# One explicit drain on GpSimd between its last load and the experts' part

## The chip, the cores and the metric

One NeuronCore of a Trainium2 chip runs the whole kernel in one launch. The metric is the device time of one execution in microseconds (us). The engines are named as the profile names them: PE (TensorE), DVE (VectorE), ACT (ScalarE), POOL (GpSimd) and SP (SyncE, which here only issues DMAs). Each engine has its own stream of instructions, and a letter q behind a name (POOLq, SPq) means the engine's sequencer: the part that reads the stream, waits on semaphores and issues DMAs.

## The reference

Eight sequences of 128 tokens with 512 features pass through one decoder layer with three parts, each followed by a layer norm without weights:

```python
x = layernorm(x + self_attention(x, Wq, Wk, Wv, Wo))      # 32 heads of 16, 8 groups, RoPE, causal
x = layernorm(x + cross_attention(x, ctx, mask, bias, ln_weight, w_q, w_k, w_v, w_out))
                                                          # 32 heads of 128; it adds x once more itself
x = layernorm(x + ffn(x))
# ffn: y = x @ W_base.T + b_base
#      + sum over 4 active experts e of alpha_e * 2 * (x @ A_e.T) @ B_e.T      (rank 8)
#      alpha = softmax(log(prior) + x @ router_W.T + router_b) over the active ones
```

## The kernel before, in words

Self-attention comes first (`self_attention`, up to L753), one sequence after the other. Cross-attention follows in 16 groups of two heads (`NG = 16`): groups 0 and 1 are written out, groups 2 to 14 (`SEVEN = 2`) are a hardware loop on each engine, and group 15 is written out again as the last one. Then comes the third part, called the experts here: the final norm of cross-attention, the base product and the low-rank experts, the last layer norm, and one store of 256 KB for each of the eight sequences.

There is no scheduler. Each engine's stream stands in the order of the Python code of its own function (`sync`, `gpsimd`, `scalar`, `vector`, `tensor` of each part), and the streams meet only in semaphores: `wait_ge(sem, n)` holds a stream until the count is reached. `nc.Block()` (opened in L909, recorded under L771) ends all five streams with the same closing sequence: each engine runs a DRAIN, tells a common semaphore, and waits until all five have arrived. An opening sequence of the same form stands before the first instruction (recorded under L2411).

What POOL does, in its order:

- In self-attention: fills, subtractions, small norm arithmetic, and two DMAs, L363 (x into `acc`) and L364 (half of the context into `stage`).
- In each group of cross-attention: four additions of bias and mask (`bias_mask`, L1048, into `bm`), four subtractions on weights (`three_turns`, `last_turn`), and seven loads of 1 MB from a scratch tensor in HBM into one of two ring buffers (`load_sums`). A load waits until PE has used what lies in the ring buffer, runs a tiny addition on the tile `pool_gate` (L1077), and issues the DMA (L1078). The loops over groups 2 to 15 issue 96 such DMAs in all.
- In the last group only `first_half(NG - 1)` is left (L1283, defined in L1263): three loads (S4k, S3q, S3k) and the additions of bias and mask for the tiles 2 and 3. The last of these, the second L1048, is POOL's last instruction in cross-attention. POOL issues no DMA after that.
- In the experts (L1284 to L1300): `rstd_x` (L1170, L1173), `add_bias` (L1178) and `rstd_y` (L1182, L1184, L1187), all of them short. The last store (L1037, issued by SP) waits for DVE's L1890, which waits for the last L1184.

SP issues all other DMAs: the weights, the bias, the experts' inputs and the eight stores. Behind them it waits until all stores have landed (L1038), and then enters the closing sequence.

Of the kernel before, what the change touches and what calls it, by code (L numbers as in the profile page):

```python
# [763 lines left out]
def layer(nc, a, sem, banks, mem, prev_a, out_d):  # L764
# [6 lines left out]
    with ExitStack() as ctx:  # L771
# [75 lines left out]
        def wait_kept(eng, name):  # L847
            i = BLOCKS.index(name)
            eng.wait_ge(s_kept[i % 2], 32 * (i // 2 + 1))
# [191 lines left out]
        def _(pool):  # L1041
            def bias_mask(g, s, first):
                n, i = TILES * g + s, heads_of(first)[s]
                if s == 0:
                    pool.wait_ge(s_bias_in, 16 * g + 16)
                if not first or s >= 2:
                    pool.wait_ge(s_nm, n - 1)
                nc.gpsimd.tensor_tensor(bm[:, s % 2], mask[:, HALF * (s // HG):HALF * (s // HG + 1), :],  # L1048
                                        bias[:, i:i + 1, :].broadcast_to([P, HALF, T]), ALU.add)\
                    .then_inc(s_bm, 1)  # L1050
# [22 lines left out]
            def load_sums(g, name, w=None, after=None):  # L1073
                k = SLOT_OF[name]
                if after is not None:
                    pool.wait_ge(s_unit[w], done(UNITS, g, after))
                    nc.gpsimd.tensor_tensor(pool_gate[:, BLOCKS.index(name):BLOCKS.index(name) + 1], eps[:, 0:1], eps[:, 0:1], ALU.add)  # L1077
                nc.gpsimd.dma_start(mem.ring[k][:].rearrange("p q c n -> p (q c n)"), sums_d[BLOCKS.index(name)])\  # L1078
                    .then_inc(s_ring[k], 16)
# [88 lines left out]
            def rstd_x(p):  # L1168
                pool.wait_ge(e_mvx, 2 * p + 2)
                nc.gpsimd.tensor_tensor(rstx[:, 2 * p:2 * p + 2], mvx[:, 2 * p:2 * p + 2, 1], eps[:], ALU.add)\  # L1170
                    .then_inc(e_vex, 1)
                pool.wait_ge(e_vex, p + 1)
                nc.gpsimd.tensor_tensor(rstx[:, 2 * p:2 * p + 2], rstx[:, 2 * p:2 * p + 2], minus_half[:], ALU.pow)\  # L1173
                    .then_inc(e_rx, 1)
# [81 lines left out]
            def second_half(g):  # L1256
                bias_mask(g, 0, False)
                last_turn(g)
                bias_mask(g, 1, False)
                load_sums(g, "S1k", 0, "p6")  # L1260
                load_sums(g, "S4q", 1, "p6")

            def first_half(g):  # L1263
                load_sums(g, "S4k", 1, "p5")
                bias_mask(g, 2, False)
                wait_kept(pool, "S4q")
                load_sums(g, "S3q", 0, "p3")
                load_sums(g, "S3k", 1, "p3")
                bias_mask(g, 3, False)
# [7 lines left out]
            with pool.Fori(SEVEN, NG - 1) as g:  # L1277
# [3 lines left out]
                load_sums(g, "S2q", 1, "p7")  # L1281
                second_half(g + 1)
            first_half(NG - 1)  # L1283
            pool.wait_ge(s_experts_in, 16 * len(EXPERT_INPUTS))  # L1284
            rstd_x(0)
            add_bias(0)
# [1134 lines left out]
```

## Time and profile before

| | |
|---|---|
| median of 3 runs | 1077.29 us (1076.80 to 1078.42) |
| the profiled execution, its own time | 1079.05 us |
| span of that execution in the trace | 1076.8 us |
| granted TensorE clock over the span, mean | 0.992 of full speed |
| PE / PEld / DVE / ACT / POOL busy | 96% / 83% / 71% / 46% / 44% |
| DMAs issued by POOL (queue q0) | 103.82 MB in 14240 packets |
| DMAs issued by SP (queue q1) | 54.37 MB in 30560 packets |

The span is what lies between the first and the last recorded instruction. The profiled execution's own time is 2.25 us longer than its span. The busy times on the page leave out register, branch, semaphore and drain instructions. Those are found by asking for the source line under which they were recorded. The answers give their times from the start of the span.

### The profile page before, as it was taken

How to read it: one execution, taken by the hardware profiler on the slowest of the kernel's cores; microseconds unless marked ns; L12 is line 12 of the kernel's file. 1: busy time of each engine (PE TensorE's matmuls, PEld its weight loads, DVE VectorE, ACT ScalarE, POOL GpSimd, SP SyncE). 2: the span in 40 equal slices, each digit the busy share in tenths (PEclk: the TensorE clock that was granted, in tenths of full speed). 3: DMA queues.
4: the chain of work that ended last, by engine and by line, in shares of the span. 5: the costliest groups of instructions: out<-in, count | busy, mean ns of one | idle time of the engine just before them, and what ended most of it. 6: DMA issues, size and time to landing. Idle time of an engine off the chain costs nothing.

```text
span 1076.8 us, 20565 instructions
## 1 busy us (share of the span) xinstructions
PE 1030.2 (96%) x6354; PEld 894.6 (83%) x6354; DVE 761.8 (71%) x2269; ACT 500.6 (46%) x1377; POOL 472.6 (44%) x567
## 2 busy tenths in 40 slices
PE   7899988999989999999999999999999999999995
PEld 6678767888778888888888888988888888988884
DVE  5799989664747676757677676767676767577883
ACT  4888886453424343534443434444343434343421
POOL 7676676599934232423324242424242424232242
PEclk9999999999999999999999999999999999999998
DMA  4302001235265556473737464646465564736001
GB/s 153 128 12 60 2 1 66 80 126 195 69 227 185 177 180 215 140 238 125 253 135 238 148 222 159 223 170 213 147 217 180 176 221 135 239 110 248 5 20 59
DMA packets 44845, 158.72 MB, mean 147 GB/s; under 512 B 4737, under 2 KB 21505, under 8 KB 32129
## 3 DMA queue, kind: packets, MB, share of 16 engines
q0 software_dynamic: 14240, 103.82, 28.0%
q1 hardware_dynamic: 30560, 54.37, 15.0%
q8 instruction: 22, 0.36, 0.1%
q14 instruction: 23, 0.18, 0.1%
HBM read 148.73 MB, written 9.44 MB: 147 GB/s over the span
## 4 chain that ended last, share of the span: by engine, by line
PE 79%; DVE 10%; issue 4%; POOL 3%; ACT 2%; DMA 2%; POOLq 0%; SPq 0%; DVEq 0%; ACTq 0%
PE bank L1946 25%; PE bank L760 20%; PE bank L2108 16%; PE bank L2095 5%; PE bank L2078 5%; PE bank L2126 3%; PE bank L2085 2%; DVE sm L481 2%; DMA ring<-block_sums 1%; POOL sm L322 1%; DVE alpha L557 1%; DMA stage<-in_wq 1%; ACT pr L1339 1%; PE bank L2164 1%; PE bank L686 1%
## 5 line engine op out<-in xcount | busy, mean ns | idle before, releaser
L1339 ACT ACTIVATE pr<-sm,nmx 128x128 f32<-128x128 f32 x256 | 99.8, 391 | 176.2 <-DVE nmx L1594 172.7
L1048 POOL TENSOR_TENSOR bm<-mask,bias 128x512 f32<-128x512 f32 x64 | 84.5, 1321 | 162.3 <-DVE nmx L1594 159.7
L1644 DVE TENSOR_TENSOR acc<-acc,bank 128x512 f32<-128x512 f32 x128 | 86.2, 684 | 80.1 <-PE bank L2108 80.1
L1077 POOL TENSOR_TENSOR pool_gate<-eps 128x1 f32<-128x1 f32 x95 | 37.6, 396 | 239.5 <-PE bank L1946 239.5
L1946 PE MATMUL bank<-ring,wqk_hi 128*128 128x512 f32 x392 | 111.0, 405 | 7.1 <-DVE wqk_lo L1612 4.1
L1612 DVE TENSOR_TENSOR wqk_lo<-qk_raw,wqk_hi 128x512 fp32r<-128x512 f32 x98 | 106.2, 1085 | 8.5 <-ACT wqk_hi L1369 8.5
L1332 ACT COPY v<-bank 128x256 f32<-128x256 f32 x124 | 45.9, 370 | 128.6 <-PE bank L760 81.8
L2108 PE MATMUL bank<-wo_hi,at_hi 128*128 128x512 f32 x256 | 101.2, 395 | 0.3 <-DVE acc L1644 0.3
L2108 PE MATMUL bank<-wo_hi,at_lo 128*128 128x512 f32 x256 | 100.5, 392 | 0.5 <-DVE at_lo L1606 0.5
L2108 PE MATMUL bank<-wo_lo,at_hi 128*128 128x512 f32 x256 | 100.6, 393 | 0.0
L1606 DVE TENSOR_TENSOR at_lo<-bank,at_hi 128x512 fp32r<-128x512 f32 x64 | 44.0, 688 | 64.5 <-ACT at_hi L1353 64.5
L760 PE MATMUL bank<-wv_hi,cT_hi 128*128 128x256 f32 x512 | 88.8, 296 | 0.2 <-DVE wv_lo L1901 0.2
L760 PE MATMUL bank<-wv_lo,cT_hi 128*128 128x256 f32 x512 | 82.3, 283 | 0.0
L760 PE MATMUL bank<-wv_hi,cT_lo 128*128 128x256 f32 x512 | 82.2, 283 | 0.0
L1946 PEld LDWEIGHTS bank<-ring,wqk_hi 128*128 128x128 f32 x392 | 67.1, 190 | 16.6 <-issue 5.1
L760 PEld LDWEIGHTS bank<-wv_hi,cT_hi 128*128 128x128 f32 x512 | 72.7, 190 | 4.6 <-issue 0.4
L1347 ACT COPY prT<-bank 128x512 f32<-128x512 f32 x64 | 37.2, 582 | 81.4 <-PE bank L2085 81.4
L2078 PEld LDWEIGHTS bank<-kT,qT 128*128 128x128 f32 x512 | 66.7, 191 | 4.8
L760 PEld LDWEIGHTS bank<-wv_hi,cT_lo 128*128 128x128 f32 x512 | 70.5, 191 | 0.0
L760 PEld LDWEIGHTS bank<-wv_lo,cT_hi 128*128 128x128 f32 x512 | 70.4, 191 | 0.0
L2095 PE MATMUL bank<-prT,v 128*128 128x128 f32 x512 | 67.8, 275 | 1.6 <-ACT prT L1347 1.6
L2078 PE MATMUL bank<-kT,qT 128*128 128x128 f32 x512 | 67.3, 274 | 0.0
(296 smaller groups left out, 2611.1 us busy)
## 6 DMA issues: line engine op xcount, KB each, us to landing
ring<-block_sums POOLq DMA_DIRECT2D x96, 1024.0 KB, 5.2
qk_raw<-in_wqk SPq DMA_DIRECT2D x56, 256.0 KB, 5.3
o_raw<-in_wo SPq DMA_DIRECT2D x16, 512.0 KB, 3.3
v_raw<-in_wv SPq DMA_DIRECT2D x15, 512.0 KB, 4.5
block_sums<-stage SPq DMA_DIRECT2D x6, 512.0 KB, 4.1
acc<-in_x POOLq DMA_DIRECT2D x1, 2048.0 KB, 8.1
qk_raw<-in_wqk SPq DMA_DIRECT2D x4, 512.0 KB, 6.3
bias<-in_bias SPq DMA_DIRECT2D x16, 128.0 KB, 2.1
```

The source lines that it names most:

```text
L760: ins = nc.tensor.matmul(out, lhs, rhs, start=start and i == 0, stop=i == len(pairs) - 1)
L1048: nc.gpsimd.tensor_tensor(bm[:, s % 2], mask[:, HALF * (s // HG):HALF * (s // HG + 1), :], bias[:, i:i + 1, :].broadcast_to([P, HALF, T]), ...
L1077: nc.gpsimd.tensor_tensor(pool_gate[:, BLOCKS.index(name):BLOCKS.index(name) + 1], eps[:, 0:1], eps[:, 0:1], ALU.add)
L1332: nc.scalar.copy(v[:, b, :], PX[b % 2][:, 0:HG * DH2]).then_inc(s_vc, 1)
L1339: e = nc.scalar.activation(pr[:, s % 2, k], sm[:, s % 2, k], ACT.Exp, bias=nmx[:, s % 2, k:k + 1], accum_out=sums[:, s % 2, k:k + 1])
L1606: nc.vector.tensor_tensor(at[1][:, s // HG, i], PO[:], f32(at[0][:, s // HG, i]), ALU.subtract).then_inc(s_al, 1)
L1612: nc.vector.tensor_tensor(part_of(slot, 1), block_of(qk_raw, raw), f32(part_of(slot, 0)), ALU.subtract).then_inc(s_op, 1)
L1644: nc.vector.tensor_tensor(acc[:, b], acc[:, b], PX[b % 2][:], ALU.add).then_inc(s_acc, 1)
L1946: ins = nc.tensor.matmul((PQ, PK)[w][:], lhs, rhs, start=i == 0, stop=i == len(pairs) - 1)
L2078: ins = nc.tensor.matmul(S[s % 2][:, tok], qT[:, s % 2, tok], kT[:, s % 2, tok], start=True, stop=True)
L2095: ins = nc.tensor.matmul(PO[:, k * T:(k + 1) * T], v[:, half * HALF + k, i * DH2:(i + 1) * DH2], prT[:, k], start=True, stop=True)
L2108: ins = nc.tensor.matmul(PX[b % 2][:], at[p][:, half, i, tok], wo[q][:, i, :], start=k == 0 and (p, q) == PARTS[0], stop=k == HG - 1 and ( ...
```

## The change

One instruction is added to POOL's stream: a DRAIN with no semaphore of its own. It stands behind the last addition of bias and mask of the last group, and ahead of the first wait of the experts.

```diff
@@ -1281,6 +1281,7 @@
                 load_sums(g, "S2q", 1, "p7")
                 second_half(g + 1)
             first_half(NG - 1)
+            pool.drain()
             pool.wait_ge(s_experts_in, 16 * len(EXPERT_INPUTS))
             rstd_x(0)
             add_bias(0)
```

All other instructions of all five streams, with their waits, stay as they are and in their order. The lines behind L1283 move down by one number.

## Rows read from the trace of the kernel before

**Rows 1.** The page: busy us, share and count of each engine; then the chain's shares.

```profile
PE 1030.2 (96%) x6354; PEld 894.6 (83%) x6354; DVE 761.8 (71%) x2269; ACT 500.6 (46%) x1377; POOL 472.6 (44%) x567
...
PE 79%; DVE 10%; issue 4%; POOL 3%; ACT 2%; DMA 2%; POOLq 0%; SPq 0%; DVEq 0%; ACTq 0%
```

**Rows 2.** The chain of waits, its last pieces: start us, us, what.

```profile
1065.37 0.45 PE bank L2176 x2
...
1067.06 0.20 POOL rstd_y L1182
...
1067.33 0.55 POOL rstd_y L1184
...
1067.92 0.59 POOLq L771
```

**Rows 3.** Line 771, the closing sequence: duration ns min/median/max, first and last start.

```profile
L771 POOLq EVENT_SEMAPHORE  x2: 17/17/17, 1076.6 to 1076.7; - x2
L771 PEldq DRAIN  x1: 2720/2720/2720, 1063.1 to 1063.1; - x1
L771 ACTq DRAIN  x1: 844/844/844, 1065.1 to 1065.1; - x1
L771 POOLq DRAIN  x1: 8684/8684/8684, 1067.9 to 1067.9; - x1
L771 DVEq DRAIN  x1: 589/589/589, 1067.9 to 1067.9; - x1
L771 SPq COMPARE_BRANCH  x1: 38/38/38, 1070.5 to 1070.5; - x1
L771 SPq DRAIN  x1: 13/13/13, 1070.7 to 1070.7; - x1
L771 SPq EVENT_SEMAPHORE  x1: 17/17/17, 1076.8 to 1076.8; - x1
...
L771 PEldq EVENT_SEMAPHORE  x1: 51/51/51, 1076.8 to 1076.8; - x1
```

**Rows 4.** Timeline of all engines from 1067 us: start us, us, engine, instruction.

```profile
1067.91 0.55 DVE L1890 TENSOR_SCALAR acc<-v_raw,mv_y,rstd_y 128x512 f32<-128x512 f32 x1 [0.94 <-POOL rstd_y L1184]
1067.97 0.53 POOL L1187 TENSOR_SCALAR minus_mean_rstd<-mv_y,rstd_y 128x1 f32<-128x1 f32 x1
1068.48 0.33 SPq L1037 DMA_DIRECT2D out<-acc  x1
```

**Rows 5.** Busy time of each engine by window, with clock, DMA share, GB/s.

```profile
1068.50:1070.70 2.20, 0.00 (x0) 0.00 (x0) 0.00 (x0) 0.00 (x0) 0.00 (x1) 0.85 0.32 119
1070.70:1076.60 5.90, 0.00 (x0) 0.00 (x0) 0.00 (x0) 0.00 (x0) 0.00 (x0) 0.50 0.00 0
```

**Rows 6.** Line 2411, the opening sequence, as in rows 3.

```profile
L2411 POOLq DRAIN  x1: 168/168/168, 0.3 to 0.3; - x1
...
L2411 POOL MEMSET const-uint8-127<- x1: 101/101/101, 0.3 to 0.3; 128x1 uint8 x1
```

**Rows 7.** Lines that issue DMAs, one by one: the form of rows 3.

```profile
L1078 POOL DMA_DIRECT2D ring<-block_sums x96: 577/577/613, 294.2 to 985.0; - x96
...
DMA to landing us min/median/max: 5.0/5.2/9.3
...
L363 POOL DMA_DIRECT2D acc<-in_x x1: 758/758/758, 43.7 to 43.7; - x1
...
L364 POOL DMA_DIRECT2D stage<-in_cT x1: 789/789/789, 44.5 to 44.5; - x1
...
L1037 SPq DMA_DIRECT2D out<-acc x8: 332/333/1570, 1044.9 to 1068.5; - x8
...
DMA to landing us min/median/max: 2.0/2.0/3.4
```

**Rows 8.** POOL's timeline around the place of the change; idle before it in brackets.

```profile
990.37 1.29 POOL L1048 TENSOR_TENSOR bm<-mask,bias 128x512 f32<-128x512 f32 x1 [4.81 <-DVE nmx L1594]
1014.71 0.19 POOL L1170 TENSOR_TENSOR rstd_x<-mv_x,eps 128x2 f32<-128x2 f32 x1 [23.05 <-DVE mv_x L1651]
```

**Rows 9.** The windows behind that place: columns as in rows 5.

```profile
991.70:999.80 8.10, 8.10 (x49) 7.00 (x48) 6.67 (x20) 4.10 (x13) 0.00 (x0) 1.00 0.57 209
999.80:1014.70 14.90, 13.37 (x91) 11.78 (x89) 11.22 (x34) 7.91 (x21) 0.00 (x0) 1.00 0.00 0
```

**Rows 10.** Line 1187, POOL's change of configuration in the experts: as rows 3.

```profile
L1187 POOLq MODIFY_POOL_CONFIG  x2: 11/11/11, 1040.1 to 1040.1; - x2
```

## The prediction

> **What bounds the kernel now.** I read the page's busy table and its chain first [rows 1]. PE is busy for 96% of the span and carries 79% of the chain, so for most of the kernel POOL's time is worth nothing: POOL is busy 44% and carries 3%. The reader should then follow the chain to its end and notice that it ends too early [rows 2]. Its last piece is POOLq at L771, from 1067.92 for 0.59 us, that is to 1068.51. The span ends at 1076.8. So 8.3 us at the end are explained by no compute row.
>
> That stretch belongs to the closing sequence, and the view of line 771 opens it [rows 3]. Five engines run a DRAIN and then meet. I add start and duration. PE is through at 1063.1 + 2.72 = 1065.8, ACT at 1065.1 + 0.84 = 1065.9, DVE at 1067.9 + 0.59 = 1068.5, and SP at 1070.7 + 0.01 = 1070.7. POOL starts at 1067.92 (the start of the last chain piece) and takes 8.684 us, to 1076.60. The meeting's semaphore instructions follow at 1076.6 to 1076.8, and that is the end. All engines are idle from 1068.5 on, and from 1070.7 to 1076.6 no byte moves [rows 5]. POOL's closing DRAIN alone holds the end for those 5.9 us.
>
> What is POOL doing in it? Its last instruction, L1187, runs from 1067.97 for 0.53 us, to 1068.50 [rows 4]. The other 8.10 us of the DRAIN (1076.60 minus 1068.50) pass with nothing of POOL's in progress. The opening DRAIN on the same engine took 168 ns, and it began beside a fill of 101 ns, both at 0.3 us [rows 6]; between 0.07 and 0.17 us of it was its own. Between the two, POOL issued 96 + 1 + 1 = 98 DMAs [rows 7]. SP issued many DMAs too, and its closing DRAIN took 13 ns, so it is POOL's kind of DMA that would count. So the trace offers one difference between the long DRAIN and the short ones: DMAs issued by POOL since the previous DRAIN. An estimate from it is 8.10 / 98 = 0.083 us for each. All of them had landed long before: the last was issued at 985.0 and the slowest of L1078 took 9.3 us [rows 7], so by 994.3. The 8.10 us would then be bookkeeping for DMAs, not waiting for data.
>
> **The change part by part.** It removes nothing, moves nothing, and adds one DRAIN on POOL.
>
> Its place: the addition ahead of it ends at 990.37 + 1.29 = 991.66, and POOL's next instruction starts at 1014.71, after 23.05 us of waiting for DVE's mv_x [rows 8]. Queued behind the DRAIN on POOL is that `rstd_x(0)` and with it everything in the experts. DVE waits for its result, and PE for DVE's. So the new DRAIN costs nothing as long as it is shorter than 23.05 us, and each us above that goes to the end one for one. Bounds of its length: below, 0.17 us (the opening one); above, by the nearest rows, 2.7 us until the slowest DMA has landed (994.3 minus 991.66) and 8.10 us of its own, 10.8 us in all. I take 8.1 us, since the same 98 DMAs stand before it. It then ends at about 999.8, with 14.9 us to spare, and the cover is the last group's work on PE and DVE [rows 9]. If that cover shrank by more than 14.9 us, the cost would begin to show.
>
> What it gives: the closing DRAIN has no POOL DMA since the previous DRAIN. Bounds of what is left of it after L1187: 0.07 us at the least (the opening DRAIN's 0.17 us less the fill beside it), 8.10 us at the most (nothing changes). I take under 0.17 us, nearest to the opening DRAIN, which had the same state: POOL arrives at about 1068.50 + 0.17 = 1068.7. Late next is SP. Its last store is issued at 1068.48 [rows 4] and takes 2.0 us to land [rows 7], so SP goes on at 1070.5 and finishes its DRAIN at 1070.7 [rows 3]. The end is then SP's, and POOL may keep up to 2.2 us of DRAIN (1070.7 minus 1068.5) without cost. Behind the last arrival come the meeting's own steps: 1076.8 minus 1076.6, 0.2 us [rows 3]. SP has to signal POOL first, where now POOL is the last itself, so I allow 0.1 us more.
>
> The sum against the profiled execution: new end 1070.7 + 0.3 = 1071.0 in place of 1076.8, a change of -5.8 us; the time goes from 1079.05 to 1073.25. The median of the runs is 1.76 us below the profiled execution, and the DRAIN is no work that depends on data, so I take the same difference there: 1077.29 - 5.8 = 1071.5 us.
>
> Could the 5.9 us be an effect of the profiler, absent in timed runs? The timed runs are only 1.76 us shorter than the profiled one. So at most that much of it could be missing from them if the rest is equal, and the gain would still be over 4.0 us.
>
> Two rules of the Trainium skill speak against a gain. The page "VectorE: DVE Perf Modes", section "The DRAIN you can't avoid", describes the drains at the two ends of a kernel as a constant of about 12 ns on all five engines. SP's 13 ns agrees; POOL's 8684 ns does not [rows 3], and the measurement decides. By that rule there would be nothing to take from the end, and the time would stay at 1077.3 us.
>
> The page "PSUM — Partial Sum Buffer", section "Engine vs sequencer instructions", says that a drain waits until its engine is fully idle. By that alone POOL would be through at 1068.5 [rows 4], 8.1 us before it is. So the trace does not agree here either, unless POOL is at work on something that has no row.
>
> **The rivals.**
>
> *No change: the 8.1 us are paid at the close in any case.* The long DRAIN differs from the opening one in more than its DMAs. It comes after 567 POOL instructions, and after a change of POOL's configuration at 1040.1 [rows 10], behind the place of the new DRAIN. If the price is one for the first DRAIN after such a change, or a fixed price once POOL has issued any DMA, the closing DRAIN stays at 8.7 us. The new one is hidden in 23.05 us either way, and the time is 1077.3 us. Against it: the compute instructions after that change ran at once, the first within 0.2 us (L1187 is 0.26 to 0.53 us in all its rows), and an engine with nothing to account for has no reason to be busy for 8 us. A rule behind this rival stands in the Trainium skill's page "GPSIMD Engine Reference", section "Instruction dispatch": the first call to freshly loaded code pays about 6 us that no row shows. No row here shows such a gap behind 1040.1.
>
> *A part only.* Some of the 8.1 us stays with the close. Up to 2.2 us of rest changes nothing; a rest of 4 us would end at 1072.5 + 0.2, and the time would be about 1073.2 us. Nothing in the trace points to a split.
>
> *Slower: the new DRAIN does its work beside DVE and holds DVE up.* At the close all other engines are idle, so rows 5 cannot show whether it disturbs them. At its new place DVE is busy for 6.67 of 8.10 us and PE for all 8.10 [rows 9]. If DVE could not run for the whole DRAIN, PE would wait for up to 8.1 us, and the sum is 8.1 - 5.8 = +2.3, 1079.6 us. The point from which it decides is 5.8 us of added time on that chain. Against it: the DRAIN has no tile to read or write, and additions of 1.3 us on POOL with two inputs each run beside DVE throughout the kernel.
>
> **How the numbers follow.** A measurement of this kernel tells 0.2% (2.15 us) from no change. The forecast, 1071.5 us, has 0.80. It is the only reading in which the sole difference in the rows matters, and it needs only that three quarters of the 8.1 us move. A part only has 0.04. No change has 0.12, because the trace holds only one long DRAIN and I can't separate its causes. Slower has 0.04. Faster by over 0.2%: 0.80 + 0.04 = 0.84; within 0.2%: 0.12; slower: 0.04. The low end takes the end at SP's arrival with the 0.2% by which two series of runs can differ: 1071.2 - 2.1 = 1069.1. The high end takes the gain of 4.0 us if the profiler has lengthened the DRAIN, 1073.3, and the partial case with some of the same spread: 1074.4. That leaves out no change and slower, 0.16.
>
> **What would show it.** Right: line 771 shows a POOLq DRAIN of about 0.6 to 0.8 us instead of 8.684, with POOL's semaphore instructions at about 1070.8; the new drain's line shows a POOLq DRAIN of about 8 us from about 990.4 or 991.7; `rstd_x` at L1170 (now one line further down) still starts at about 1014.7, released by DVE; PE's last product ends where it did, at 1065.8. Wrong: two long DRAINs (the price is fixed); a short new one and a long closing one (the cause lies behind 990); wider gaps on PE between 992 and 1015 (contention).

## The result, and the profile after

The changed kernel takes 1072.1 us in the median of 5 runs (1071.17 to 1072.34), against 1077.29 us for the kernel before (5 runs as well, with the same median as the 3 above). The ratio is 0.995, with a 95% interval from 0.9935 to 0.9964, so it is clear of 1. A second series on one chip gave 0.9944 [0.9931, 0.9957]. The profiled execution took 1072.06 us with a span of 1069.9 us.

The closing sequence, line 771, in the changed kernel answers to [rows 3]. Columns: duration in ns min/median/max, first and last start.

```profile
L771 POOLq EVENT_SEMAPHORE  x2: 17/17/17, 1069.7 to 1069.8; - x2
L771 PEldq DRAIN  x1: 2718/2718/2718, 1062.1 to 1062.1; - x1
L771 ACTq DRAIN  x1: 844/844/844, 1064.0 to 1064.0; - x1
L771 POOLq DRAIN  x1: 664/664/664, 1066.9 to 1066.9; - x1
L771 DVEq DRAIN  x1: 586/586/586, 1066.9 to 1066.9; - x1
...
L771 SPq DRAIN  x1: 13/13/13, 1069.6 to 1069.6; - x1
L771 SPq EVENT_SEMAPHORE  x1: 17/17/17, 1069.8 to 1069.8; - x1
```

POOL's closing DRAIN is down from 8684 to 664 ns. SP is now the last to arrive, and 0.2 us later all is over. From the start of PE's closing DRAIN to the end it took 1076.8 - 1063.1 = 13.7 us before and takes 1069.9 - 1062.1 = 7.8 us now: 5.9 us less.

The new DRAIN in the same trace (line 1284), then POOL's timeline around it, which answers to [rows 8]. The code behind the change stands one line further down.

```profile
L1284 POOLq DRAIN  x1: 9432/9432/9432, 989.1 to 989.1; - x1
```

```profile
989.13 1.29 POOL L1048 TENSOR_TENSOR bm<-mask,bias 128x512 f32<-128x512 f32 x1 [4.80 <-DVE nmx L1595]
1013.63 0.19 POOL L1170 TENSOR_TENSOR rstd_x<-mv_x,eps 128x2 f32<-128x2 f32 x1 [23.21 <-DVE mv_x L1652]
```

The DRAIN begins beside the addition, which ends at 990.42, and is through at 989.1 + 9.43 = 998.6. Its own part is 8.1 us, as long as what the closing DRAIN had paid. `rstd_x` is still released by DVE.

The span fell by 6.9 us, 1.0 us more than the end explains. At the addition L1048, ahead of the new DRAIN, the changed kernel is already 990.37 - 989.13 = 1.2 us early. The five runs of the same kernel have spans from 1069.0 to 1070.2 us, so this is within their scatter. The traces show where the scatter sits. These are the sixteenth of the 64 additions of bias and mask, in the kernel before and then in the changed one:

```profile
379.97 1.28 POOL L1048 TENSOR_TENSOR bm<-mask,bias 128x512 f32<-128x512 f32 x1 [4.08 <-DVE nmx L1594]
...
378.74 1.28 POOL L1048 TENSOR_TENSOR bm<-mask,bias 128x512 f32<-128x512 f32 x1 [4.09 <-DVE nmx L1595]
```

The 1.2 us are there already. From this addition to the last one it is 990.37 - 379.97 = 610.40 us before and 989.13 - 378.74 = 610.39 us now. In all other traces below whose loads are as they were, and that have no DRAIN between these two additions, it is 610.38 to 610.40 us too, while the sixteenth starts anywhere from 377.5 to 380.0 us. So a cost or a gain late in the kernel can be read from such stretches to a few hundredths of a microsecond, and better than from the whole time.

Did the DRAIN disturb its neighbours? This is the window of its 8.1 us in the changed kernel, against the first of [rows 9]. Columns: busy us of PE, PEld, DVE, ACT, POOL, then clock, DMA share, GB/s.

```profile
990.42:998.56 8.14, 8.14 (x48) 6.95 (x47) 6.52 (x20) 3.99 (x12) 0.00 (x1) 1.00 0.57 207
```

PE is busy throughout in both and DVE does 20 instructions in both, in 6.52 us now and 6.67 us before. DMAs moved 207 GB/s and 209 GB/s. From the start of the addition to `rstd_x` it takes 1014.71 - 990.37 = 24.34 us before and 1013.63 - 989.13 = 24.50 us now. Two of the kernels below have no DRAIN in this stretch either, and it takes 24.37 and 24.58 us in them. So no delay by the DRAIN shows.

### The profile page after: what moved, and what is told of

Same layout as the page of the kernel before. It is cut to its first block, busy times and chain, and to the rows that moved or that the text cites. A ratio compares the mean times of both kernels' runs of the same rounds, so it can differ in the third digit from the quotient of the medians.

```text
span 1069.9 us, 20566 instructions
## 1 busy us (share of the span) xinstructions
PE 1028.4 (96%) x6354; PEld 893.1 (83%) x6354; DVE 760.8 (71%) x2269; ACT 501.1 (47%) x1377; POOL 473.0 (44%) x567
## 4 chain that ended last, share of the span: by engine, by line
PE 78%; DVE 10%; issue 5%; POOL 3%; ACT 2%; DMA 1%; POOLq 0%; DVEq 0%; ACTq 0%
PE bank L1947 25%; PE bank L760 20%; PE bank L2109 16%; PE bank L2096 5%; PE bank L2079 5%; PE bank L2127 3%; PE bank L2086 2%; DVE sm L481 2%; DMA ring<-block_sums 1%; POOL sm L322 1%; DVE alpha L557 1%; ACT pr L1340 1%; PE bank L2165 1%; PE bank L686 1%; DVE mn L481 1%
## 5 line engine op out<-in xcount | busy, mean ns | idle before, releaser
L1048 POOL TENSOR_TENSOR bm<-mask,bias 128x512 f32<-128x512 f32 x64 | 85.0, 1329 | 162.1 <-DVE nmx L1595 159.5
```

## The experiments

All of them start from the kernel before, unless the edit says otherwise. Where a DRAIN's own part is given, it is its duration less what still ran of the instruction ahead of it. For the closing one that is L1187 or its like, which ends 0.59 us after the DRAIN begins. The diffs are cuts, and some of the code in them is shortened.

### One DRAIN pays, the next does not

```diff
+            pool.drain()
             pool.drain()          # the changed kernel, with a second one
```

> Two DRAINs in a row at the place of the change. Theory (a DRAIN pays about 0.083 us for each POOL DMA issued since the previous one): the first takes 8.1 us of its own (about 9.4 with the addition of 1.29 us ahead of it), the second under 0.2 us, the closing one 0.66 us as after the change, and the time is that of the changed kernel, 1072 us. Rival (a fixed price of each DRAIN once POOL has issued DMAs, which the closing one escapes for another reason): the second takes 8 us too, still within the 23 us of waiting.

Its single run took 1070.8 us. The two DRAINs, lines 1284 and 1285:

```profile
L1284 POOLq DRAIN  x1: 9432/9432/9432, 987.9 to 987.9; - x1
...
L1285 POOLq DRAIN  x1: 47/47/47, 997.4 to 997.4; - x1
```

The second costs 47 ns. There is no fixed price of each DRAIN; there is a debt, and the first one clears it.

### The same DRAIN at the end saves nothing

```diff
             for b in range(2, B):
                 rstd_y(b)
+            pool.drain()
```

> The same DRAIN, but as POOL's last instruction, behind the last rstd_y. Theory (the work is moved, not saved): the explicit DRAIN takes 8.1 us of its own behind POOL's last instruction, the closing one under 0.2 us, and the end is where it was before the change: 1077.3 us, ratio 1.000. Rival (any additional DRAIN makes the closing one short and costs little itself): 1072 us, ratio 0.995.

1077.32 us, ratio 1.000 [0.9988, 1.0013]. Lines of the closing sequence, and the explicit DRAIN (line 1301):

```profile
L771 SPq DRAIN  x1: 13/13/13, 1068.7 to 1068.7; - x1
L771 POOLq DRAIN  x1: 47/47/47, 1074.7 to 1074.7; - x1
...
L1301 POOLq DRAIN  x1: 8682/8682/8682, 1066.0 to 1066.0; - x1
```

The explicit one takes what the closing one took before, 8682 against 8684 ns, and SP waits for it as before. What gains is the place, not the instruction.

### 95 DMAs ahead of the DRAIN, 3 behind it

```diff
+            pool.drain()
             first_half(NG - 1)
```

> The DRAIN stands ahead of the three loads of the last group, with 95 DMAs issued before it and 3 behind it. Theory per DMA: the explicit one takes 95 x 0.083 = 7.9 us of its own; POOL has about 4.4 us of waiting there (the gap ahead of S4k), so that load and what uses it come 3 to 4 us late, and the closing DRAIN pays for 3 DMAs, 0.25 us behind L1187, still ahead of SP. Time: between 1072 us (PE does not need the load at once) and 1076 us. Rival (a fixed price whenever any POOL DMA is outstanding): the closing DRAIN is 8.7 us again and the time 1077 to 1081 us.

1074.82 us, ratio 0.9982 [0.9969, 0.9995]. The two DRAINs, then where PE waits, then the windows around it:

```profile
L771 POOLq DRAIN  x1: 908/908/908, 1069.3 to 1069.3; - x1
...
L1283 POOLq DRAIN  x1: 9061/9061/9061, 968.7 to 968.7; - x1
```

```profile
PE bank L1947 <- DMA ring<-block_sums: 2.9, 1, 2.9
```

```profile
980.50:983.45 2.95, 0.03 (x1) 0.00 (x1) 0.00 (x0) 0.37 (x1) 0.32 (x1) 1.00 1.05 397
983.45:987.40 3.95, 3.95 (x10) 3.13 (x11) 1.31 (x5) 0.00 (x0) 0.71 (x2) 0.57 0.51 193
```

The closing DRAIN is 908 ns here and 664 ns in the changed kernel. The difference, 0.24 us, is the price of the 3 DMAs behind the explicit DRAIN: 0.081 us each. The explicit one ends at 968.7 + 9.06 = 977.7, and the issue ahead of it at 969.3. So its own part for 95 DMAs is 8.4 us, where 7.9 us were expected: half a microsecond more, directly behind a load just issued. It delays the load S4k, PE waits 2.9 us for it, and in the next 4 us its granted clock is 0.57, near the lower of its two levels, after a stretch with hardly any work. At that clock the stretch does what takes 2.3 us at full speed, so 1.7 us more went there, and a gap of 0.4 us that PE has in this group in the kernel before is gone. By these rows 2.9 + 1.7 - 0.4 = 4.2 us were lost of the 5.9 us gained; by the medians (1074.82 against 1076.78 us in this series) 2.0 us are left, so 3.9 were lost.

### More DMAs for the same bytes

The two kernels split loads over the partitions. In the first of them only S1k and S4k are split (`PIECES_OF` is 2 for these), in the second all seven. The counts that PE waits for grow to match. In the cut `ring` and `sums` stand for the two sides of the copy.

```diff
-                nc.gpsimd.dma_start(ring, sums).then_inc(s_ring[k], 16)
+                for h in range(PIECES_OF[name]):
+                    part = slice(h * P // PIECES_OF[name], (h + 1) * P // PIECES_OF[name])
+                    nc.gpsimd.dma_start(ring[part], sums[part]).then_inc(s_ring[k], 16)
```

> No explicit DRAIN. Only the loads S1k and S4k are issued as two DMAs of 64 partitions each: 28 more, 126 POOL DMAs in all, the same bytes, packets up by 16 for each split load (448, 3%). It stays below the count of about 130 at which the split kernel seemed to settle. Theory per DMA: the closing DRAIN pays 126 x 0.083 = 10.4 us behind L1187. Rival (by packets or bytes): 8.1 to 8.4 us. Rival (a fixed price): 8.1 us.

The closing DRAIN with 126 DMAs, and the queue's packets and megabytes:

```profile
L771 POOLq DRAIN  x1: 10976/10976/10976, 1079.6 to 1079.6; - x1
...
q0 software_dynamic: 14688, 103.82, 32.6%
```

Its own part is 10.976 - 0.59 = 10.39 us, 0.082 us for each of 126. Packets grew by 3% and bytes not at all, so by either it would have been 8.4 us at most. Up to here the price goes by the DMA. (These kernels are slower for other reasons too, 1093.1 us here, 1112.3 us and 1079.4 us for the next two. Only their closing DRAIN is read.)

> No explicit DRAIN. Each of the 96 loads of 1 MB is issued as two DMAs of 512 KB over 64 partitions each: 194 POOL DMAs, the same bytes, and nearly the same number of packets. Theory per DMA: the closing DRAIN takes 194 x 0.083 = 16.1 us behind L1187, and the span is about 8 us longer by that alone, besides what the additional 96 issues of 0.58 us cost in the groups. Rival (the price goes by bytes or packets): it stays at 8.1 us. Rival (a fixed price): also 8.1 us.

This one missed. With 194 DMAs the closing DRAIN is shorter, not longer:

```profile
L771 POOLq DRAIN  x1: 6234/6234/6234, 1103.6 to 1103.6; - x1
```

Its own part is 5.65 us, the price of about 68 DMAs. Before the 131st DMA POOL paused for 1.53 us with nothing named as the cause. In the kernel before, POOL's idle time of this kind ahead of all 96 loads comes to 0.5 us in two places. POOL's timeline at the pause:

```profile
789.39 0.19 POOL L1077 TENSOR_TENSOR pool_gate<-eps 128x1 f32<-128x1 f32 x1 [3.81 <-PE bank L1948]
791.10 1.06 POOL L1080 DMA_DIRECT2D ring<-block_sums  x2 [1.53 <-issue]
```

The idea that the queue settles old DMAs by itself at some point was formed on this, and tried by splitting over the columns instead (128 partitions and half of the columns in each part).

> No explicit DRAIN. Each of the 96 loads is issued as two DMAs of 512 KB over all 128 partitions and half of the columns: 194 POOL DMAs with about 28,000 packets, where the split by partitions had 194 with 15,776 and its closing DRAIN paid 5.65 us. Theory now (0.083 us per DMA, but at about 130 DMAs without a DRAIN the queue settles its old ones by itself, so only some 66 to 68 are left at the close): 5.6 us again. Rival (the price goes by packets): 5.65 x 28,000 / 15,776 = 10 us.

The closing DRAIN in this kernel, and POOL's timeline at its only pause:

```profile
L771 POOLq DRAIN  x1: 7382/7382/7382, 1069.6 to 1069.6; - x1
...
714.30 0.54 POOL L1080 DMA_DIRECT2D ring<-block_sums  x1 [0.86 <-issue]
```

The closing DRAIN's own part is 6.79 us: the price of 82 DMAs. Neither number expected came out. The only pause of more than 0.3 us of this kind (0.86 us) stood before the 116th DMA. In both kernels the DMAs from the pause on (64 and 79) are 3 or 4 fewer than those paid for, which fits a queue that clears most of its debt in that pause. What decides when it does so was not found. The first kernel had issued some 10,700 packets by then (416 for the two early DMAs and 80 for each half load) and the second some 16,700 (144 for each half load), so neither a number of DMAs nor a number of packets fits both. And the pause is far shorter than a DRAIN for as many DMAs. This stays open. The kernel before, with 98 DMAs, shows no such pause.

### A DRAIN in each turn of the loop

```diff
                 load_sums(g, "S2q", 1, "p7")
+                pool.drain()
                 second_half(g + 1)
             first_half(NG - 1)
+            pool.drain()
```

> A DRAIN in each turn of the loop, behind the load S2q (7 POOL DMAs since the previous one, 9 or 10 in the first turn), and the one of the change. Theory: 7 x 0.083 = 0.6 us each, or about 1.1 us with what POOL still has to do for the load just issued; POOL then waits for DVE's nmx anyway (1.8 us), so the loop is no longer, the last explicit DRAIN pays for 5 DMAs (0.4 us), and the time is 1072 us. Rival (a DRAIN waits until the DMA before it has landed, 5.2 us): each DRAIN takes about 5 us, bias and mask come 3 us late in 13 groups, and the time goes up by as much as 13 x 3 = 39 us if all of it shows.

1070.33 us, ratio 0.9935 [0.9919, 0.9952]. The loop's 13 DRAINs (line 1282), the last explicit one, and POOL's timeline in one turn:

```profile
L1282 POOLq DRAIN  x13: 7327/7393/7752, 333.5 to 943.1; - x13
...
L1285 POOLq DRAIN  x1: 1819/1819/1819, 987.4 to 987.4; - x1
```

```profile
945.10 0.58 POOL L1078 DMA_DIRECT2D ring<-block_sums  x1
950.78 1.29 POOL L1048 TENSOR_TENSOR bm<-mask,bias 128x512 f32<-128x512 f32 x1 [5.11 <-issue]
```

The size expected for the loop was wrong, and the rival was right about it. The DRAIN that starts at 943.1 ends at 950.5, and the load issued at 945.10 lands 5.1 us later, at 950.2. It is so in every turn: the DRAIN ends 0.3 to 0.4 us after the load ahead of it has landed. In the one turn in which that load took 5.5 us, from 538.65 to 544.1, the DRAIN is the longest of the 13, 7752 ns, and ends at 544.4. With few DMAs to account for, a DRAIN directly behind a load waits for it to land. The loss that the rival expected did not follow: the addition behind it starts 5.7 us after the load's issue (950.78 and 945.10) instead of 2.4 us (950.37 and 948.02 in the kernel before), and had room for that. Of the 96 loads two stand ahead of the loop, 91 in it and 3 behind it; with the two early DMAs that makes 9 for the first turn's DRAIN. The last DRAIN pays 1.82 - 1.34 = 0.48 us for the 5 DMAs since the last turn, again about 0.08 us each plus a few hundredths.

Is this faster than the changed kernel? Both were run side by side:

> The changed kernel itself, for a direct comparison with the next one on the same chip: ratio 0.995 to the kernel before (0.9945 to 0.995 in the runs so far).

> The kernel with a DRAIN in each turn of the loop, once more. Its 13 DRAINs took 7.4 us each (6.5 us behind POOL's last row), not 0.6 us, and its ratio was 0.9935 [0.9919, 0.9952]. If the DRAINs in the loop help or cost nothing but scatter: 0.9945 to 0.995, the same as the changed kernel within 0.1%. If they bring something of their own: 0.9935, 1.6 us under it.

0.9944 [0.9931, 0.9957] for the changed kernel and 0.9939 [0.9926, 0.9952] with the DRAINs in the loop. The intervals overlap almost wholly, and no difference was found. The traces say the same. In the first trace with the DRAINs in the loop the sixteenth and the last addition of bias and mask are these:

```profile
377.04 1.28 POOL L1048 TENSOR_TENSOR bm<-mask,bias 128x512 f32<-128x512 f32 x1 [4.08 <-DVE nmx L1596]
...
987.44 1.29 POOL L1048 TENSOR_TENSOR bm<-mask,bias 128x512 f32<-128x512 f32 x1 [4.80 <-DVE nmx L1596]
```

Between them lie 610.40 us, as without these DRAINs. What made this execution short is the early start of the sixteenth addition, and in the second trace of the same kernel that addition starts at 379.57. So as far as the kept traces show, the first ratio of the loop was scatter ahead of its turns.

### Two other places

```diff
             load_sums(NG - 1, "S3k", 1, "p3")     # first_half written out
+            pool.drain()
             bias_mask(NG - 1, 3, False)
```

> One DRAIN directly behind the issue of the last load S3k and ahead of the last addition of bias and mask, where POOL waits for 4.8 us only. Theory: it takes 98 x 0.083 = 8.1 us, up to 8.6 us behind a fresh issue, so that addition comes 3.3 to 3.8 us late. In the kernel with the DRAIN ahead of the last group a delay of 4 us cost about 2.7 us of the gain; so 1073 to 1076 us. Rival (only the place before the close matters, POOL's addition has slack): 1072 us.

1071.97 us, ratio 0.9945 [0.9928, 0.9962]. The new DRAIN (line 1288), and the addition behind it:

```profile
L1288 POOLq DRAIN  x1: 9433/9433/9433, 985.0 to 985.0; - x1
...
994.50 1.28 POOL L1048 TENSOR_TENSOR bm<-mask,bias 128x512 f32<-128x512 f32 x1 [8.78 <-issue]
```

The expected length came out: it ends at 994.4, 8.7 us after the issue's end at 985.72. The load ahead of it landed 5.2 us after its start, at 990.3, 4 us before the DRAIN's end. So here the wait for the landing ran while the debt of 98 DMAs was paid: the two do not add up, and behind a fresh load the 98 cost 8.7 us and not 8.1. The expected time missed and the rival held: the addition starts 9.4 us after the load's issue instead of 5.4 us (994.50 and 985.14 here, 989.13 and 983.75 in the changed kernel), and nothing is lost. From that load to `rstd_x` it is 29.8 us here (1014.92 - 985.14) and 29.9 us in the changed kernel (1013.63 - 983.75). The addition had at least 4 us of slack. (The loss of 2.7 us that the expectation takes from the kernel with the DRAIN ahead of the last group compares medians of two series; within one series it was 3.9 us, as said there.)

```diff
             rstd_x(0)
+            pool.drain()
             add_bias(0)
```

> The DRAIN stands 25 us later, between rstd_x(0) and add_bias(0). Theory (8.1 us of its own, exposed where POOL has no such wait): add_bias(0) starts 6.9 us late, at about 1023.8 instead of 1016.9, and the second rstd_x 6.2 us late; PE has its base products to do meanwhile, so 3 to 6 us of it show on PE, and the gain of 5.9 us at the end is eaten: 1074 to 1077 us. Rival (POOL has slack in the experts too): 1072 us.

1079.22 us, ratio 1.0016 [1.0005, 1.0026]: slower than before the change. The direction was right, the size was not. POOL, then PE, then two windows in this kernel:

```profile
1021.64 2.48 POOL L1178 TENSOR_TENSOR acc<-qk_raw,stage 128x512 f32<-128x512 f32 x2 [8.19 <-issue]
```

```profile
1025.70 1.97 PE L2121 MATMUL bank<-ident,qk_raw 128*128 128x128 f32 x8 [5.96 <-DVE qk_raw L1659]
```

```profile
1019.70:1025.70 6.00, 0.04 (x2) 0.01 (x1) 0.60 (x2) 0.00 (x0) 3.34 (x4) 0.70 0.00 0
1025.70:1029.10 3.40, 3.40 (x13) 3.07 (x14) 2.47 (x5) 1.17 (x2) 2.76 (x2) 0.52 0.00 0
```

POOL's delay of 6 to 7 us reaches PE as a wait of 6.0 us. I had counted on PE's base products to cover a part, but they stand behind the transposes that wait (L2121). Then the clock adds to it. After 6 us almost without work PE was granted 0.52 of full speed for 3.4 us, close to the lower of its two levels (1.2 of 2.4 GHz). At half speed that stretch does what takes about 1.8 us at full speed, so 1.6 us more went there. Together 7.6 us. From `rstd_x` at 1012.47 to PE's closing DRAIN at 1068.4 it takes 55.9 us, against 1063.1 - 1014.71 = 48.4 us before, which is 7.5 us more. Against a gain of 5.9 us that is 1.6 to 1.7 us slower; the medians of the series differ by 1079.22 - 1077.62 = 1.6 us.

## Why the prediction was right

*The end is held by POOL's closing DRAIN alone.* Shown: with the debt cleared early, the stretch behind PE's last product shrank by 5.9 us, and with the DRAIN as POOL's last instruction it did not shrink.

*The cause is DMAs issued by POOL since the previous DRAIN, not the instructions nor the change of configuration at 1040.1.* Shown by number: 3 DMAs 0.24 us, 98 DMAs 8.10 us, 126 DMAs 10.39 us, between 0.081 and 0.083 us each, which is the estimate of 0.083 us. The closing DRAIN of the changed kernel, with none to pay for, still takes 664 ns, of which 0.07 us are its own. Measured from there the price is 0.082 us for each of 98 (8684 - 664 ns), 0.082 for each of 126 (10976 - 664) and 0.081 for each of 3 (908 - 664). The rival that the close pays in any case fell with that same DRAIN of 664 ns: between the new DRAIN and the closing one still stand the change of configuration, now at 1039.0, and POOL's 40 instructions of the experts.

```profile
L1187 POOLq MODIFY_POOL_CONFIG  x2: 11/11/11, 1039.0 to 1039.0; - x2
```

A fixed price of each DRAIN fell with the second one of 47 ns, and one that any DMA sets off with the 0.24 us for 3. With 194 DMAs the proportion no longer holds, for a reason left open; the kernel in question has 98. What POOL does for each DMA in this time no row shows. That it is bookkeeping stays the prediction's reading, and the runs show only that all loads had landed long before (in the kernel before the last was issued at 985.0 and took 5.1 us, and the closing DRAIN began at 1067.9).

*The new DRAIN takes 8.1 us and is covered.* It took 8.1 us of its own and ended 15 us before POOL was needed. That the place mattered is shown by the DRAIN in the experts, 25 us later, which turned the gain into a loss. The rule of "one for one" was too mild where PE then idles: the granted clock behind the wait made about 7.5 us out of 6.0.

*SP is late next.* It arrived at 1069.6, and the end followed within 0.3 us, as allowed for. POOL keeps 0.07 us after L1187, at the lower bound. That bound was not a true one: a DRAIN with nothing ahead of it took 47 ns. Nothing hangs on this, as SP comes 2 us later.

*Contention with DVE.* It does not show: 20 DVE instructions took 6.52 us beside the DRAIN and 6.67 us without it, and the stretch from the addition to `rstd_x` is as long with the DRAIN in it (24.50 us) as in the three kernels without (24.34 to 24.58 us).

*The sizes.* -5.8 us was forecast. The medians differ by 5.2 us, 1077.29 - 1072.1, the series on one chip by 5.7 us, and the traces show 5.9 us at the end. So the gain is in the medians too, and not only in the profiled execution. The rest is scatter between runs, which the traces show in the first 380 us, far ahead of the change.

## What to carry to other kernels

When a chain of waits ends before the span does, ask for the line of the closing sequence and compare the engines' DRAINs: the last to arrive sets the end. An engine that issued DMAs through the software queue (`q0 software_dynamic` on the page) may owe time for each of them, here 0.082 us, to be paid in its next DRAIN. Pay it once, behind its last DMA, at a place where that engine waits for longer than the debt and no load, addition or transpose stands behind it that PE needs sooner; a place where PE has to idle costs more than the wait.

## What the runs showed that was not expected

A DRAIN behind a load just issued waited until it had landed (7.4 us in each turn of the loop), even with only 7 DMAs to account for; with 98 to account for, the landing was over before the DRAIN was. With 194 DMAs the price at the close was lower than with 126 (5.65 and 6.79 us against 10.39 us), with one pause of 1.53 or 0.86 us at an issue in mid-kernel. And the additions of bias and mask had 4 us of slack, though POOL waits 4.8 us for DVE ahead of the last one.
